# Expert tiles of a mixture of experts: the turn of the silu rows moved ahead of the next tile's gate and up products

## The chip, the cores and the metric

The kernel runs on one NeuronCore of a Trainium2 chip: TensorE (matmuls), VectorE, ScalarE, GpSimd and SyncE, which here issues most transfers. The metric is the time of one execution on the device in microseconds (us), lower is better.

## What is computed

A whole two-layer network runs in one launch: attention, feed-forward, attention and feed-forward, then a gated delta net, a mixture of experts, a linear recurrence, and the same mixture again. The change touches the mixture alone, which runs twice (`moe1`, `moe2`), on 2048 rows of 256 numbers, in float32:

```python
logits = x @ router_w
expert_idx = jnp.argmax(logits, axis=-1)
score = jax.nn.sigmoid(jnp.max(logits, axis=-1))
xs = x * score[:, None]
for e in range(n_experts):                       # 8 experts, D = F = 256
    m = (expert_idx == e)[:, None]
    xe = jnp.where(m, xs, 0.0)
    h = jax.nn.silu(xe @ gate_w[e]) * (xe @ up_w[e])
    out = out + jnp.where(m, h @ down_w[e], 0.0)
shared = jax.nn.silu(x @ shared_gate_w) * (x @ shared_up_w) @ shared_down_w
```

## The kernel before

`route_and_sort` finds each row's expert, scales the rows by the score, and scatters them with indirect transfers into a DRAM tensor `moe_xs`, sorted by expert and padded, so that each tile of 128 rows belongs to one expert. There are SL = 23 such tiles (16 full ones and 7 for the padding). Then each tile goes through its expert, and the results, in the DRAM tensor `moe_ys`, are gathered back. The shared expert of batches 0 and 1 runs ahead of the tiles (`hidden`, `down`, lines 798 to 816), that of batches 2 and 3 behind them (line 890), while GpSimd gathers (line 943).

One tile q takes these steps:

- a load of 128 KB from `moe_xs` into `moe_rows` (L783), issued by SyncE; three buffers;
- on TensorE the turn of the rows, `turn_rows` (L839, 2 matmuls against the identity), copied to `moe_rows_turned` by VectorE (L1009);
- on TensorE gate and up together, `gate_up` (L849: 4 matmuls of 512 columns in the trace); ScalarE takes the silu of the gate half (L917), VectorE multiplies it by the up half into `moe_hidden` (L1015);
- on TensorE the turn of that product, `turn_hidden` (L861, 2 matmuls), copied to `moe_hidden_turned` by ScalarE (L922);
- on TensorE the down product, `result` (L871: 4 matmuls of 256 columns), copied to `moe_result` by ScalarE (L926), and a store of 128 KB to `moe_ys` (L778), issued by SyncE.

The order on every engine is written out by hand and skewed over tiles. Each engine runs its own instructions in that order, and semaphores join the engines. TensorE's iteration q (lines 878 to 886) is: load the tile's expert number into a register, turn the rows of tile q, gate and up of tile q-1, turn the hidden rows of tile q-2, result of tile q-2. The wait ahead of `turn_hidden` is for the product of its tile (`hr`, L855), the wait ahead of `result` is for the copy of its turned rows (`htc`, L865). SyncE's iteration q (lines 780 to 785) waits until the rows of tile q-3 are turned, issues the load of tile q, then waits for the copied result of tile q-3 and issues its store. So the load of tile q+1 stands behind the store of tile q-3 in SyncE's queue. VectorE alternates the copy of tile q's turned rows with the product of tile q-1 (lines 1004 to 1015).

Of the kernel before, what the change touches and what calls it, by code (L numbers as in the profile page):

```python
# [16 lines left out]
KT = DM // P  # L17
# [708 lines left out]
def route_and_sort(nc, name, X, XN, XT, W, M, C):  # L726
# [4 lines left out]
    E, F = 8, DM  # L731
    SL = NT + E - 1
    xs_d, ys_d = M.xs_d, M.ys_d
    with Stage(nc, name) as s:
# [16 lines left out]
        HRT = [s.sb(f"hidden_turned{i}", [P, KT, P]) for i in range(2)]  # L751
# [3 lines left out]
        xtp, gup, htp, yp = B[0:2], B[2:4], B[4:6], B[6:8]  # L755
# [11 lines left out]
        @blk.sync  # L767
        def _(sp):
            sp.dma_start(rw[:, :, :], tiles(W["router"])).then_inc(ld, 16)
            sp.dma_start(tri[:, :], C.dram["before"]).then_inc(ld, 16)  # L770
            sp.dma_start(thr[:, :], C.dram["thresholds"]).then_inc(ld, 16)  # L771
            sp.dma_start(slots[:, :], C.dram["slots"]).then_inc(ld, 16)  # L772
            if M.load is not None:
                M.load(sp)

            def store(q):
                sp.wait_ge(yc, q + 1)
                sp.dma_start(ys_d[q * P:(q + 1) * P, :], YR[q % 3][:, :]).then_inc(yst[q % 3], 16)  # L778
            sp.wait_ge(scat, 16 * NT)
            for q in range(SL):  # L780
                if q >= 3:
                    sp.wait_ge(xt, q - 2)
                sp.dma_start(XR[q % 3][:, :], xs_d[q * P:(q + 1) * P, :]).then_inc(rld[q % 3], 16)  # L783
                if q >= 3:
                    store(q - 3)
            for q in range(SL - 3, SL):
                store(q)

        @blk.tensor
        def _(pe):  # L790
# [41 lines left out]
            def turn_rows(q):  # L832
                pe.wait_ge(rld[q % 3], 16 * (q // 3 + 1))
                if q < 2:
                    pe.wait_ge(silus, 2 * FIRST - 1 + q)
                else:
                    pe.wait_ge(xtc, q - 1)
                for k in range(KT):
                    mm = nc.tensor.transpose(xtp[q % 2][:, k * P:(k + 1) * P], XR[q % 3][:, k * P:(k + 1) * P], C.ident[:, :])  # L839
                mm.then_inc(xt, 1)  # L840

            def gate_up(q, e):
                if q < 2:
                    pe.wait_ge(hids, 2 * FIRST - 1 + q)
                else:
                    pe.wait_ge(hr, q - 1)
                pe.wait_ge(xtc, q + 1)
                for k in range(KT):
                    mm = nc.tensor.matmul(gup[q % 2][:, :], XRT[q % 2][:, k, :],  # L849
                                          M.wgu[:, k, ds(e, 1), :].rearrange("p a n -> p (a n)"),  # L850
                                          start=(k == 0), stop=(k == KT - 1))
                mm.then_inc(gu, 1)

            def turn_hidden(q):
                pe.wait_ge(hr, q + 1)  # L855
                if q < 2:
                    pe.wait_ge(added, TB * (FIRST - 1) + q + 1)
                else:
                    pe.wait_ge(htc, q - 1)
                for k in range(KT):  # L860
                    mm = nc.tensor.transpose(htp[q % 2][:, k * P:(k + 1) * P], HR[q % 2][:, k * P:(k + 1) * P], C.ident[:, :])  # L861
                mm.then_inc(ht, 1)

            def result(q, e):
                pe.wait_ge(htc, q + 1)  # L865
                if q < 2:
                    pe.wait_ge(added, TB * (FIRST - 1) + q + 3)
                else:
                    pe.wait_ge(yc, q - 1)
                for f in range(KT):  # L870
                    mm = nc.tensor.matmul(yp[q % 2][:, 0:DM], HRT[q % 2][:, f, :],  # L871
                                          M.wd[:, f, ds(e, 1), :].rearrange("p a n -> p (a n)"),
                                          start=(f == 0), stop=(f == KT - 1))
                mm.then_inc(yd, 1)
# [3 lines left out]
            for q in range(SL + 2):  # L878
                if q < SL:
                    chosen[q] = pe.value_load(EXP[0:1, q:q + 1], min_val=0, max_val=E - 1)  # L880
                    turn_rows(q)
                if 1 <= q <= SL:
                    gate_up(q - 1, chosen[q - 1])
                if q >= 2:
                    turn_hidden(q - 2)
                    result(q - 2, chosen[q - 2])
            pe.wait_ge(hr, SL)
            pe.wait_ge(xtc, SL)
# [7 lines left out]
        @blk.scalar  # L896
        def _(act):
            act.wait_ge(bested, 1)
            nc.scalar.activation(score[:, :], best[:, :], ACT.Sigmoid).then_inc(scored, 1)
            act.wait_ge(scored, 1)  # L900
            for t in range(NT):
                nc.scalar.activation(XN[:, t, :], XN[:, t, :], ACT.Copy, scale=score[:, t:t + 1]).then_inc(xsd, 1)

            def silu(b):
                for f in range(2):
                    act.wait_ge(gates, 2 * b + f + 1)
                    if b > 0:
                        act.wait_ge(hids, 2 * (b - 1) + f + 1)
                    nc.scalar.activation(act_sb[f][:, :], gp[f][:, :], ACT.Silu).then_inc(silus, 1)
            for b in range(FIRST):  # L910
                silu(b)
            for q in range(SL + 2):
                if 1 <= q <= SL:
                    act.wait_ge(gu, q)
                    if q >= 3:
                        act.wait_ge(hr, q - 2)
                    nc.scalar.activation(SG[(q - 1) % 2][:, :], gup[(q - 1) % 2][:, 0:F], ACT.Silu).then_inc(sg, 1)  # L917
                if q >= 2:
                    act.wait_ge(ht, q - 1)
                    if q >= 4:  # L920
                        act.wait_ge(yd, q - 3)
                    nc.scalar.copy(HRT[q % 2][:, :, :], htp[q % 2][:, 0:F].rearrange("p (k n) -> p k n", k=KT)).then_inc(htc, 1)  # L922
                    act.wait_ge(yd, q - 1)
                    if q >= 5:
                        act.wait_ge(yst[(q - 2) % 3], 16 * ((q - 2) // 3))
                    nc.scalar.copy(YR[(q - 2) % 3][:, :], yp[q % 2][:, 0:DM]).then_inc(yc, 1)  # L926
            for b in range(FIRST, BATCH):
                silu(b)
# [1576 lines left out]
```

## Time and profile before

| | us |
|---|---|
| median of 3 runs | 4703.91 |
| lowest, highest | 4699.47, 4708.26 |
| the profiled execution, whole | 4706.56 |
| its span | 4704.8 |
| tiles of `moe1` in it, first turn to the last result's start | 4210.02 to 4303.80 |
| tiles of `moe2` in it | 4568.26 to 4660.33 |

A row of the profile names a line, an engine, an operation and the tensors (out <- in). PE is TensorE's matmuls, PEld its weight loads, DVE VectorE, ACT ScalarE, SPq the transfers that SyncE issues. A matmul of 256 columns lasts 379 ns from start to end, and its successor starts before it ends, so distances between starts tell more of TensorE than durations do. The granted clock of TensorE is a share of 2.4 GHz: 1.00 is that level, 0.50 is 1.2 GHz.

### The profile page before, as it was taken

How to read it: one execution, taken by the hardware profiler on the slowest of the kernel's cores; microseconds unless marked ns; L12 is line 12 of the kernel's file. 1: busy time of each engine (PE TensorE's matmuls, PEld its weight loads, DVE VectorE, ACT ScalarE, POOL GpSimd, SP SyncE). 2: the span in 40 equal slices, each digit the busy share in tenths (PEclk: the TensorE clock that was granted, in tenths of full speed). 3: DMA queues.
4: the chain of work that ended last, by engine and by line, in shares of the span. 5: the costliest groups of instructions: out<-in, count | busy, mean ns of one | idle time of the engine just before them, and what ended most of it. 6: DMA issues, size and time to landing. Idle time of an engine off the chain costs nothing. (4 is left out here: it accounts for less than half of the span.)

```text
span 4704.8 us, 79644 instructions
## 1 busy us (share of the span) xinstructions
PE 4118.0 (88%) x27938; PEld 2752.2 (58%) x27938; DVE 2696.7 (57%) x7063; ACT 2268.6 (48%) x6183; POOL 630.6 (13%) x557
## 2 busy tenths in 40 slices
PE   5988988888797799959999999999999999977667
PEld 3555545555555566646666666666766666644344
DVE  3663357777623788856666665566556666423342
ACT  1551146666411566635556555656565565522111
POOL 0000010000000344421111111111111111111011
PEclk8788989889897899979999999999999999979879
DMA  2000100000000655553222332333233232121012
GB/s 70 1 1 24 51 1 2 2 2 2 4 27 5 206 200 205 213 134 84 79 70 74 84 84 71 81 84 83 70 84 84 66 80 79 37 92 57 11 34 76
DMA packets 402161, 318.92 MB, mean 68 GB/s; under 512 B 289200, under 2 KB 339056, under 8 KB 399728
## 3 DMA queue, kind: packets, MB, share of 16 engines
q1 hardware_dynamic: 398704, 305.53, 22.6%
q0 software_dynamic: 3072, 8.39, 0.6%
q8 instruction: 225, 3.69, 0.3%
q14 instruction: 160, 1.31, 0.1%
HBM read 195.94 MB, written 117.88 MB: 67 GB/s over the span
## 5 line engine op out<-in xcount | busy, mean ns | idle before, releaser
L2153 ACT ACTIVATE d_heads_VP<-d_heads_chain,d_GALL 128x128 f32<-128x128 f32 x512 | 187.9, 367 | 665.1 <-PE d_heads_chain L2055 663.5
L2299 DVE SCALAR_TENSOR_TENSOR d_heads_S<-d_heads_S,d_GALL,d_heads_chain 128x128 f32<-128x128 f32 x768 | 232.4, 344 | 436.0 <-PE d_heads_chain L2060 435.9
L599 ACT ACTIVATE b_heads_PR<-b_heads_sc,b_heads_NM 128x384 f32<-128x384 f32 (+3 forms) x512 | 273.0, 535 | 203.4 <-DVE b_heads_NM L667 203.4
L1763 DVE SCALAR_TENSOR_TENSOR d_front_CY<-d_front_proj,d_CW,d_front_CY 128x511 f32<-128x511 f32 (+2 forms) x384 | 274.1, 745 | 72.6 <-ACT d_front_CY L1681 68.0
L1969 PE MATMUL d_heads_value<-all_XT,d_heads_WVZ 128*128 128x512 f32 x512 | 271.1, 612 | 27.9 <-DMA d_heads_WVZ<-w_d_qkvz 27.9
L2232 POOL TENSOR_TENSOR d_heads_RM<-d_heads_MS,d_heads_mhalf 128x4 f32<-128x4 f32 x128 | 130.4, 1019 | 1199.9 <-DVE d_heads_MS L2312 1199.9
L2277 DVE SCALAR_TENSOR_TENSOR d_heads_CY<-d_heads_value,d_CW,d_heads_CY 128x511 f32<-128x511 f32 (+2 forms) x384 | 284.6, 741 | 1.8
L1990 PE MATMUL d_heads_value<-d_heads_WVZ,all_XT 128*128 128x256 f32 x1024 | 273.6, 390 | 12.0 <-DVE d_heads_CY L2277 12.0
L2087 PE MATMUL d_heads_projected<-d_heads_WO,d_heads_OT 128*128 128x256 f32 x1024 | 277.0, 394 | 0.7 <-ACT d_heads_OT L2172 0.7
L2060 PE MATMUL d_heads_chain<-d_heads_VP,d_heads_KD 64*128 64x128 f32 x1792 | 220.4, 322 | 54.2 <-ACT d_heads_VP L2153 54.1
L2291 DVE SCALAR_TENSOR_TENSOR d_heads_UU<-d_heads_chain,d_GALL,d_heads_VB 128x128 f32<-128x128 f32 x448 | 156.5, 349 | 192.9 <-PE d_heads_chain L2042 192.9
L547 PEld LDWEIGHTS b_heads_tp<-all_ident,b_heads_PR 128*128 128x128 f32 x1280 | 158.0, 156 | 170.7 <-ACT b_heads_PR L599 129.1
L2042 PE MATMUL d_heads_chain<-d_heads_S,d_heads_KQ 128*64 128x128 f32 x1792 | 249.3, 302 | 8.5 <-DVE d_heads_S L2299 2.4
L547 PE MATMUL b_heads_tp<-all_ident,b_heads_PR 128*128 128x128 f32 x1280 | 223.6, 311 | 37.2 <-DVE b_heads_PT L679 24.3
L1639 PE MATMUL d_front_proj<-all_XT,d_front_WKQ 128*128 128x512 f32 x512 | 242.4, 618 | 15.3 <-DMA d_front_WKQ<-w_d_qkvz 15.3
L2065 PE MATMUL d_heads_output<-d_heads_VP,d_heads_ITB 128*128 128x128 f32 x1024 | 244.4, 321 | 0.0
L538 PE MATMUL b_heads_sc<-b_QKT,b_heads_QM 32*128 32x128 f32 (+3 forms) x1024 | 229.3, 527 | 17.0 <-DVE b_heads_QM L635 8.9
L2060 PEld LDWEIGHTS d_heads_chain<-d_heads_VP,d_heads_KD 64*128 64x128 f32 x1792 | 134.8, 184 | 176.9 <-ACT d_heads_VP L2153 163.7
L2227 POOL TENSOR_TENSOR d_heads_QS<-d_heads_KQ,d_heads_GE 128x512 f32<-128x512 f32 x128 | 162.9, 1274 | 517.2 <-PE d_heads_output L2065 510.8
L2045 PE MATMUL d_heads_output<-d_heads_S,d_heads_QS 128*64 128x128 f32 x1792 | 226.8, 282 | 0.0
L2263 DVE TENSOR_TENSOR d_heads_TMP<-d_heads_INV 128x30 f32<-128x30 f32 (+14 forms) x480 | 209.5, 437 | 28.5 <-DMA d_heads_INV<-d_l 25.1
L2042 PEld LDWEIGHTS d_heads_chain<-d_heads_S,d_heads_KQ 128*64 128x64 f32 x1792 | 126.7, 136 | 158.5 <-DVE d_heads_S L2299 56.2
(323 smaller groups left out, 8932.3 us busy)
## 6 DMA issues: line engine op xcount, KB each, us to landing
d_kq<-d_front_KQ SPq DMA_DIRECT2D x64, 768.0 KB, 4.3
d_heads_KQ<-d_kq SPq DMA_DIRECT2D x64, 768.0 KB, 4.9
d_heads_GE<-d_gerows SPq DMA_DIRECT2D x128, 256.0 KB, 5.3
d_front_GR<-d_grows SPq DMA_DIRECT2D x32, 512.0 KB, 6.4
d_it<-d_front_LI SPq DMA_DIRECT2D x64, 256.0 KB, 2.1
d_l<-d_front_LI SPq DMA_DIRECT2D x64, 256.0 KB, 4.0
d_heads_ITB<-d_it SPq DMA_DIRECT2D x128, 128.0 KB, 2.8
d_heads_INV<-d_l SPq DMA_DIRECT2D x256, 32.0 KB
```

What stands on the lines that cost most here:

```text
L547: mm = nc.tensor.transpose(TP[j][:, k * P:(k + 1) * P], PR[p % 3][j][:, k * P:(k + 1) * P], C.ident[:, :])
L599: nc.scalar.activation(PR[p % 3][j][:, 0:width(p)], SC[p % 2][j][:, 0:width(p)], ACT.Exp, bias=NM[:, u % 2, t, slot:slot + 1], scale=-1.0 ...
L1639: mm = nc.tensor.matmul(FB[2 * (i % 2) + c][:, :], WKQ[:, k, g, col:col + HD], XT[:, k, b * SEQ:(b + 1) * SEQ], start=(k == 0), stop=(k == ...
L1763: stt(y, FB[2 * (i % 2) + c][:, 0:SEQ - j], CW[:, n, 3 - j:4 - j], y, ALU.mult, ALU.add).then_inc(convstep if j < 3 else convs, 1)
L1969: mm = nc.tensor.matmul(BV[h][:, :], w[:, k, h * HD:(h + 1) * HD], XT[:, k, b * SEQ:(b + 1) * SEQ], start=(k == 0), stop=(k == KT - 1))
L1990: mm = nc.tensor.matmul(BV[t // 2][:, (t % 2) * DM:(t % 2 + 1) * DM], XT[:, k, b * SEQ + t * P:b * SEQ + (t + 1) * P], w[:, k, 2 * HD:4 * HD],
L2042: mm = nc.tensor.matmul(R[0][hrows(h), 0:HD], kq[:, c, 0, :], S[:, h, :], start=True, stop=True)
L2060: mm = nc.tensor.matmul(R[h][:, HD:2 * HD], KD[i % 2][hrows(h), c, :], VP[c % 2][hrows(h), :], start=True, stop=True)
L2065: mm = nc.tensor.matmul(inter, ITB[i % 2][:, c, :], VP[c % 2][:, :], start=(c == 0), stop=True, skip_group_check=True)
L2087: mm = nc.tensor.matmul(BO[:, t * DM:(t + 1) * DM], OT[:, h, t * P:(t + 1) * P], WO[g % 2][:, h, :], start=(h == 0), stop=(h == 1))
L2277: stt(y, BV[h][:, 0:SEQ - j], CW[:, 2 * HK + 2 * g + h, 3 - j:4 - j], y, ALU.mult, ALU.add).then_inc(convstep if j < 3 else convs, 1)
L2299: stt(S[:, h, :], S[:, h, :], gate(i, GEL0 + h, c), R[h][:, HD:2 * HD], ALU.mult, ALU.add).then_inc(su, 1)
```

## The change

On TensorE, `turn_hidden(q - 2)` moves from behind `gate_up(q - 1)` to ahead of it. On ScalarE, the copy of the turned hidden rows of tile q-2 moves from behind the silu of tile q-1 to ahead of it; the copy of the result stays last. Waits move with their instructions; none is added or dropped. VectorE, SyncE and GpSimd keep their order. In the changed file lines behind the edit stand one or two further down: L918 is the copy that was L922, L923 the silu that was L917, L928 the copy that was L926.

```diff
@@ -879,10 +879,11 @@
                     turn_rows(q)
+                if q >= 2:
+                    turn_hidden(q - 2)
                 if 1 <= q <= SL:
                     gate_up(q - 1, chosen[q - 1])
                 if q >= 2:
-                    turn_hidden(q - 2)
                     result(q - 2, chosen[q - 2])
@@ -910,16 +911,17 @@
             for q in range(SL + 2):
+                if q >= 2:
+                    act.wait_ge(ht, q - 1)
+                    if q >= 4:
+                        act.wait_ge(yd, q - 3)
+                    nc.scalar.copy(HRT[q % 2][:, :, :], htp[q % 2][:, 0:F].rearrange("p (k n) -> p k n", k=KT)).then_inc(htc, 1)
                 if 1 <= q <= SL:
                     act.wait_ge(gu, q)
                     if q >= 3:
                         act.wait_ge(hr, q - 2)
                     nc.scalar.activation(SG[(q - 1) % 2][:, :], gup[(q - 1) % 2][:, 0:F], ACT.Silu).then_inc(sg, 1)
                 if q >= 2:
-                    act.wait_ge(ht, q - 1)
-                    if q >= 4:
-                        act.wait_ge(yd, q - 3)
-                    nc.scalar.copy(HRT[q % 2][:, :, :], htp[q % 2][:, 0:F].rearrange("p (k n) -> p k n", k=KT)).then_inc(htc, 1)
                     act.wait_ge(yd, q - 1)
```

On TensorE, in one iteration of the tile loop, the difference of the two orders (L880 loads the expert's number, the ISA rows set the weights' address from it):

```order
 L880 ISA x2
 L839 MATMUL moe_bank<-all_ident,moe_rows 128x128 x2
-L849 ISA
-L849 MATMUL moe_bank<-moe_gate_up,moe_rows_turned 128x512
-L849 ISA
-L849 MATMUL moe_bank<-moe_gate_up,moe_rows_turned 128x512
 L861 MATMUL moe_bank<-all_ident,moe_hidden 128x128 x2
+L849 ISA
+L849 MATMUL moe_bank<-moe_gate_up,moe_rows_turned 128x512
+L849 ISA
+L849 MATMUL moe_bank<-moe_gate_up,moe_rows_turned 128x512
 L871 ISA
 L871 MATMUL moe_bank<-moe_down,moe_hidden_turned 128x256
```

The gate and up products of the next tile now stand between the turn of the hidden rows (L861) and the result that needs their copy (L871); the two turns stand side by side.

On ScalarE, the first tiles of a call before:

```order
L917 ACTIVATE moe_gate_silu<-moe_bank 128x256 x2
L922 COPY moe_hidden_turned<-moe_bank 128x256
L926 COPY moe_result<-moe_bank 128x256
L917 ACTIVATE moe_gate_silu<-moe_bank 128x256
L922 COPY moe_hidden_turned<-moe_bank 128x256
L926 COPY moe_result<-moe_bank 128x256
```

And the same place after:

```order
L923 ACTIVATE moe_gate_silu<-moe_bank 128x256
L918 COPY moe_hidden_turned<-moe_bank 128x256
L923 ACTIVATE moe_gate_silu<-moe_bank 128x256
L928 COPY moe_result<-moe_bank 128x256
L918 COPY moe_hidden_turned<-moe_bank 128x256
L923 ACTIVATE moe_gate_silu<-moe_bank 128x256
L928 COPY moe_result<-moe_bank 128x256
```

The copy for the result comes ahead of the next tile's silu, in the order in which TensorE now feeds the two.

## Rows read from the trace of the kernel before

**Rows 1.** The page: busy time (share, instructions), and the last chain's start by line.

```profile
PE 4118.0 (88%) x27938; PEld 2752.2 (58%) x27938; DVE 2696.7 (57%) x7063; ACT 2268.6 (48%) x6183; POOL 630.6 (13%) x557
...
PE moe_bank L849 1%; PE moe_bank L871 1%; PE moe_bank L804 0%; PE moe_bank L814 0%; ACT moe_hidden_turned L922 0%; PE moe_bank L839 0%; DMA moe_rows<-moe_xs 0%; DVE all_X L1025 0%; ACT moe_gate_silu L917 0%; DVEq L37 0%; ACT moe_result L926 0%; SPq L770 0%; DVE all_X L999 0%; SPq L772 0%; SPq L771 0%
```

**Rows 2.** Line L871: what TensorE sat idle for before it (us, times).

```profile
  ACT moe_hidden_turned L922: 27.9, 46
```

**Rows 3.** Timeline of one tile in `moe2`: start us, duration, engine, line [idle before].

```profile
4615.68 0.38 PE L839 MATMUL moe_bank<-all_ident,moe_rows 128*128 128x128 f32 x2
...
4615.88 0.37 ACT L926 COPY moe_result<-moe_bank 128x256 f32<-128x256 f32 x1 [1.30 <-PE moe_bank L871]
4615.90 1.92 PE L849 MATMUL moe_bank<-moe_gate_up,moe_rows_turned 128*128 x4
...
4616.28 0.32 SPq L778 DMA_DIRECT2D moe_ys<-moe_result  x1
...
4616.65 0.43 SPq L783 DMA_DIRECT2D moe_rows<-moe_xs  x1
...
4617.66 0.38 PE L861 MATMUL moe_bank<-all_ident,moe_hidden 128*128 128x128 f32 x2
...
4617.86 0.38 ACT L917 ACTIVATE moe_gate_silu<-moe_bank 128x256 f32<-128x256 f32 x1 [1.61 <-PE moe_bank L849]
4618.14 0.37 ACT L922 COPY moe_hidden_turned<-moe_bank 128x256 f32<-128x256 f32 x1
4618.28 0.42 DVE L1015 TENSOR_TENSOR moe_hidden<-moe_gate_silu,moe_bank 128x256 f32<-128x256 f32 x1 [1.75 <-ACT moe_gate_silu L917]
...
4618.65 1.13 PE L871 MATMUL moe_bank<-moe_down,moe_hidden_turned 128*128 x4 [0.60 <-ACT moe_hidden_turned L922]
...
4619.61 0.38 PE L839 MATMUL moe_bank<-all_ident,moe_rows 128*128 128x128 f32 x2
```

**Rows 4.** Timelines of the shared expert: a stream without waits, and VectorE releasing TensorE.

```profile
4319.39 5.34 PE L814 MATMUL moe_bank<-moe_shared_down,moe_hid 128*128 128x256 f32 x24
...
4560.29 0.42 DVE L999 TENSOR_TENSOR all_X<-all_X,moe_bank 128x256 f32<-128x256 f32 x1 [2.45 <-PE moe_bank L814]
...
4560.77 0.73 PEld L814 LDWEIGHTS moe_bank<-moe_shared_down,moe_hid 128*128 128x128 f32 x4 [0.34 <-DVE all_X L999]
```

**Rows 5.** Landing of the loads of L783: all 46, and those issued at 4604.86 and 4632.36.

```profile
DMA to landing us min/median/max: 1.9/2.2/3.5
...
DMA to landing us min/median/max: 2.7/2.7/2.7
...
DMA to landing us min/median/max: 3.5/3.5/3.5
```

**Rows 6.** Timeline of the head of the loop in `moe2`.

```profile
4568.26 1.41 PE L839 MATMUL moe_bank<-all_ident,moe_rows 128*128 128x128 f32 x4 [3.52 <-DMA moe_rows<-moe_xs]
...
4572.51 0.38 PE L839 MATMUL moe_bank<-all_ident,moe_rows 128*128 128x128 f32 x2
...
4573.13 0.42 DVE L1015 TENSOR_TENSOR moe_hidden<-moe_gate_silu,moe_bank 128x256 f32<-128x256 f32 x1 [3.00 <-ACT moe_gate_silu L917]
...
4576.40 0.38 PE L839 MATMUL moe_bank<-all_ident,moe_rows 128*128 128x128 f32 x2
```

**Rows 7.** TensorE's timeline: turns of tiles 3 and 22 in `moe1`, 22 in `moe2`, its last result.

```profile
4219.78 0.38 PE L839 MATMUL moe_bank<-all_ident,moe_rows 128*128 128x128 f32 x2
...
4295.21 0.38 PE L839 MATMUL moe_bank<-all_ident,moe_rows 128*128 128x128 f32 x2
...
4651.68 0.38 PE L839 MATMUL moe_bank<-all_ident,moe_rows 128*128 128x128 f32 x2
...
4660.33 1.12 PE L871 MATMUL moe_bank<-moe_down,moe_hidden_turned 128*128 x4 [0.61 <-ACT moe_hidden_turned L922]
```

**Rows 8.** Stretches: from:to, length, busy us of PE, PEld, DVE, ACT, POOL; clock, DMA share, GB/s.

```profile
4219.80:4299.10 79.30, 67.21 (x241) 37.16 (x241) 16.91 (x40) 20.39 (x60) 0.00 (x0) 1.00 0.21 65
4568.00:4576.30 8.30, 7.38 (x20) 3.63 (x20) 2.82 (x8) 1.03 (x3) 0.00 (x0) 0.77 0.12 41
4576.30:4655.60 79.30, 66.77 (x242) 37.59 (x241) 16.93 (x40) 20.39 (x60) 0.00 (x0) 1.00 0.21 65
```

## The prediction, made before the changed kernel ran

> **What bounds the kernel now.** I began with the page: TensorE is busy 88% of the span, and the chain that ended last runs through the expert tiles by way of TensorE and ScalarE's copy L922 [rows 1]. That share is a mean over many stages, so I went to the stage that the change touches, and there to what ended TensorE's waits. Ahead of `result` (L871) TensorE sat idle 27.9 us in all, 46 times, until ScalarE's copy of the turned hidden rows was there [rows 2]: once per tile, 2 calls of 23 tiles.
>
> One tile's timeline shows why [rows 3]. The turn L861 starts at 4617.66, the copy L922 at 4618.14, and the result at 4618.65: 0.99 us from turn to result, of which the turn itself needs 0.22 (the other turn, L839, holds its successor back from 4615.68 to 4615.90). TensorE has nothing to do in between. The other steps by their starts: turn of rows 0.22, gate and up 1.76 (4615.90 to 4617.66), result 0.96 (4618.65 to 4619.61). Sum 0.22 + 1.76 + 0.99 + 0.96 = 3.93 us, the distance of the two turns shown. From the turn of tile 3 to that of tile 22 are 19 such distances: 75.43 us in `moe1`, 75.28 in `moe2` [rows 6, 7], 3.97 and 3.96 each. Behind the tiles both TensorE (the shared expert) and GpSimd (the gather) wait for the last tile's result, so what the loop saves leaves the path that sets the end.
>
> **What the change removes.** With gate and up between turn and result, the copy has 0.22 + 1.76 = 1.98 us of TensorE's work to hide under and needs 0.99: the wait ahead of the result goes, with 0.99 us of slack. The result, no longer started from idle, should also lose its slow start: 24 such matmuls without a wait take 5.34 us [rows 4], (5.34 - 0.38) / 23 = 0.216 apart, so 4 take 0.86 instead of 0.96. TensorE alone then needs 0.22 + 0.22 + 1.76 + 0.86 = 3.06 us a tile. If the slow start stays it is 3.16.
>
> **What is late next.** Three things move with it, and each has to be paid from rows.
>
> First, the turn of the hidden rows now needs its product sooner. Before, a whole gate-and-up product lay between; now only the result and the turn of rows do. From the start of gate and up: silu at 1.96 (4615.90 to 4617.86), product 0.42 later, 0.42 long [rows 3], and VectorE's end to TensorE's start 0.06 (4560.71 to 4560.77) [rows 4]: 2.86 us. TensorE reaches the turn at 1.76 + 0.86 + 0.22 = 2.84. So it waits some 0.02 us, and this loop closes at 2.86 + 0.22 = 3.08 us a tile. It is a tie; each 0.1 us by which the path is longer than read costs 0.1 a tile. What is queued behind this wait on TensorE is gate and up of the next tile.
>
> Second, the loads. SyncE issues the load of tile q+1 behind the store of tile q-3: 0.97 us after that tile's result gave way to the next turn (4615.68 to 4616.65) [rows 3]; it lands 2.2 us later at the median [rows 5], and TensorE needs it one iteration on. With 0.05 for the release that is 3.22 us, against 3.93 of cover before and 3.06 to 3.08 after: 0.15 short. A turn that comes late does not delay the result that stands before it, so the next load is issued as early as ever and finds a longer cover: late and punctual turns alternate, and the mean is (3.08 + 3.22) / 2 = 3.15. This transfer was not waited for in a usual tile, so its price is bounded: 3.08 if every load lands in 2.1 us or less, (3.08 + 1.02 + 2.7) / 2 = 3.40 if every load takes the 2.7 that the second slowest takes [rows 5]. I take 2.2, the median of 46, since two transfers of 128 KB a tile keep the engines busy only 0.21 of the time [rows 8]. Every second tile then restarts from idle, for up to 0.10: 3.15 + 0.05 = 3.20 us a tile.
>
> The Trainium skill ("DMA: Bandwidth & Descriptors", Anatomy of one DMA) puts a near constant 2.0 us on a transfer, and its fit (for transfers that GpSimd issues) would give 2.3 for 128 KB; with it the mean would be 3.20 before the restart, 2 us more over both calls. The trace's median is 2.2.
>
> Third, ScalarE's order. The silu now stands behind the wait for the turn, but the turn comes 1.98 us ahead of the silu's own input, so nothing is late. The copy of the result runs from 0.20 to 0.57 after the turn of rows starts [rows 3], the next copy of hidden rows is due at 0.22 + 0.48 = 0.70: no conflict. The expert number's load into TensorE's register now runs ahead under gate and up as before under the result: nothing. VectorE and GpSimd keep order and load: nothing.
>
> **Head and tail.** In iteration 2 the turn of tile 0's hidden rows must wait for a product that ends at 4573.13 + 0.42 = 4573.55 [rows 6]: TensorE idles from 4572.73 to 4573.61. The next turn of rows then comes at 4573.61 + 0.22 + 1.76 + 0.86 = 4576.45, against 4576.40: 0.05 us lost and no gain for that tile. At the end, from the turn of tile 22 to the last result were 8.65 us (4651.68 to 4660.33) [rows 7]. Now: two turns 0.44, gate and up to the next hidden turn 2.86, turn 0.22, again 2.86, and the last turn to result 0.99, uncovered as before: 7.37. That saves 1.28.
>
> **The sum.** 19 distances in each call: 75.43 + 75.28 - 38 x 3.20 = 150.7 - 121.6 = 29.1. Tails 2 x 1.28 = 2.6, heads -0.1. A load of 3.5 us, one in this execution [rows 5], costs up to 0.9 more than before, as its cover shrank by that: -0.9. Together 30.7 us. The profiled execution took 4706.56, which gives 4675.9; it lies 2.65 above the median of the three runs, so against that median I forecast 4673.2.
>
> **Rivals.** (A) The loads set the pace: with less cover and stores of the same rate, landings go to 2.5 to 2.7 us. For it: single loads of 2.7 and 3.5 exist, and both 128 KB transfers now come every 3.2 us. Against: DMA share 0.21. At 3.40 a tile: 150.7 - 129.2 + 1.6 = 23.1, so 4680.8. (B) A wait in place of the one removed: the product reaches the turn later than 2.86, say 0.25 us late each time, 3.33 a tile: 150.7 - 126.5 + 1.6 = 25.8, so 4678.1. The tie speaks for it; that each step of the path is read from rows speaks against more. (C) It does nothing that can be measured: that needs 3.9 - 0.25 = 3.7 us a tile, a path from gate and up to turn of 3.5, 0.6 us longer than its rows. Time 4697 to 4704. (D) Slower, through the clock. TensorE's first turns, after 3.52 us of idle, ran long (1.41 us for 4, against 0.38 for 2), and the granted clock of the head was 0.77, that of the steady stretches 1.00 with 0.60 us of idle in each tile [rows 6, 8]. The change puts 0.88 us of idle into the head, just where the clock has come up from its lower level, 1.2 GHz. If that level returned and stayed, a tile would need about 2 x 3.06 = 6.1 us, 2.15 more than now and 2.9 more than forecast: from 30.7 / 2.9, some 11 of the 46 tiles on, the kernel is slower; with 16, 4703.9 - 30.7 + 46.4 = 4720. Against it: 0.60 us of idle per tile leaves 1.00 granted, and the change ends most idle time.
>
> The Trainium skill ("TensorE: Matmul & The Clock Gate", Part 1) says that the throttled clock is the default and activity releases it, which by itself would favour a loop with fewer gaps. The trace agrees on the busy stretches, which were granted 1.00.
>
> **How the numbers follow.** Forecast (3.08 to 3.28 a tile) 0.72, A 0.12, B 0.09, C 0.05, D 0.02. Range: its low end is TensorE alone at 3.06, 150.7 - 116.3 + 2.5 = 36.9, so 4667, less some 2 for the runs' own spread of 4.4 either way; its high end takes in A and B, 4681, with 4 for the spread and 2 for both at once. 4665 to 4687. A measurement of this kernel can tell about 0.2%, 9.4 us, from no change; faster by more than that is the forecast with A and B, 0.93, no change 0.05, slower 0.02.
>
> **What would show it.** In the profile after, turns of rows 3.1 to 3.3 us apart, L871 with no idle time but at each call's last tile (under 2 us in all for 46), L839 waiting for `moe_rows` loads about every second tile by 0.1 to 0.3, L861 waiting for VectorE's product by under 0.1. Rival A shows as landings over 2.4 in the median and waits at L839 of 0.4 and more; B as waits at L861 of 0.2 and more; C as turns still 3.8 apart; D as a granted clock under 1.00 in the tiles. I am wrong if the loop stays above 3.4.

## The result and the profile after

| kernel | median, us | lowest to highest | runs | profiled run | its span | granted clock |
|---|---|---|---|---|---|---|
| before | 4701.69 | 4696.35 to 4708.26 | 4 | 4706.56 | 4704.8 | 0.919 |
| after | 4661.17 | 4657.25 to 4669.32 | 4 | 4669.32 | 4667.5 | 0.919 |

The ratio is 0.9915, 95% interval 0.9896 to 0.9935: faster, by 40.5 us or 0.85%. I had forecast 4673.2 in a range of 4665 to 4687. The sign was right; the time lies 3.8 us below the range.

The profile answers first on the loop. On the page, TensorE is busy 12 us less than before, its weight loads as long as before, and the span is 37 us shorter [rows 1]; ScalarE's copy of the turned hidden rows, which stood high in the chain, is gone from the lines that the page shows of it.

```profile
PE 4106.2 (88%) x27938; PEld 2751.5 (59%) x27938; DVE 2696.8 (58%) x7063; ACT 2273.0 (49%) x6183; POOL 629.5 (13%) x557
...
PE moe_bank L849 1%; PE moe_bank L871 0%; POOL moe_xs L939 0%; PE moe_bank L794 0%; POOL all_XN L945 0%; PE moe_bank L804 0%; DMA moe_rows<-moe_xs 0%; PE moe_bank L839 0%; PE moe_bank L861 0%; DVE all_X L1027 0%; DMA all_XN<-moe_ys,moe_pos 0%; DMA moe_xs<-all_XN,moe_pos 0%; DMA moe_slots<-c_slots 0%; DMA moe_ys<-moe_result 0%; DVE moe_hidden L1017 0%
```

What TensorE sat idle for (us, times), ahead of the result L871, of the turn of hidden rows L861 and of the turn of rows L839, one line of each line's own view:

```profile
  ACT moe_hidden_turned L918: 1.1, 2
```

```profile
  DVE moe_hidden L1017: 5.2, 8
```

```profile
  DMA moe_rows<-moe_xs: 42.6, 42
```

The 27.9 us ahead of the result [rows 2] are 1.1, and those belong to the last tile of each call. L861 waits only in the first and the last tiles of the calls. L839 waited for loads 21.7 us, 8 times, before; now it is 42.6 us, 42 times. That view counts a weight load (PEld) and its matmul apart: 35 of the 46 turns of rows show such a wait, 5 did before. The loads have become what is late.

One tile and the start of the next in `moe2`, start and duration in us, in the form of [rows 3]:

```profile
4599.81 0.44 PE L839 MATMUL moe_bank<-all_ident,moe_rows 128*128 128x128 f32 x2
...
4600.09 0.38 PE L861 MATMUL moe_bank<-all_ident,moe_hidden 128*128 128x128 f32 x2
...
4600.31 1.88 PE L849 MATMUL moe_bank<-moe_gate_up,moe_rows_turned 128*128 x4
...
4600.51 0.37 ACT L918 COPY moe_hidden_turned<-moe_bank 128x256 f32<-128x256 f32 x1 [0.17 <-PE moe_bank L861]
...
4600.73 0.43 SPq L783 DMA_DIRECT2D moe_rows<-moe_xs  x1
...
4602.03 1.03 PE L871 MATMUL moe_bank<-moe_down,moe_hidden_turned 128*128 x4
...
4602.64 0.42 DVE L1017 TENSOR_TENSOR moe_hidden<-moe_gate_silu,moe_bank 128x256 f32<-128x256 f32 x1 [1.93 <-ACT moe_gate_silu L923]
...
4602.90 0.20 PEld L839 LDWEIGHTS moe_bank<-all_ident,moe_rows 128*128 128x128 f32 x2 [0.25 <-DMA moe_rows<-moe_xs]
4602.91 0.44 PE L839 MATMUL moe_bank<-all_ident,moe_rows 128*128 128x128 f32 x2
...
4603.18 0.38 PE L861 MATMUL moe_bank<-all_ident,moe_hidden 128*128 128x128 f32 x2
```

The copy L918 starts at 4600.51 and is needed at 4602.03, so it lies under gate and up. Turn to turn is 4602.91 - 4599.81 = 3.10 us, where [rows 3] had 3.93. The product ends at 4602.64 + 0.42 = 4603.06, 0.12 before the next L861.

The stages by the starts of the turns. "Ahead" is the part of the program before the first turn of `moe1`, which no kernel here changes; a call runs from its first turn to the start of its last result; a distance is the mean of the 19 from tile 3 to tile 22.

| profile | ahead | distance `moe1` / `moe2` | tail, each call | both calls | last result to end | span |
|---|---|---|---|---|---|---|
| before | 4210.0 | 3.970 / 3.962 | 8.59 / 8.65 | 185.85 | 44.47 | 4704.8 |
| after | 4208.4 | 3.201 / 3.268 | 7.44 / 7.44 | 154.66 | 40.38 | 4667.5 |
| e1, before again | 4214.0 | 3.972 / 3.968 | 8.59 / 8.66 | 184.85 | 40.33 | 4701.2 |
| e2, after again | 4205.7 | 3.352 / 3.182 | 7.43 / 7.44 | 155.88 | 40.34 | 4666.3 |
| e7, after | 4212.9 | 3.359 / 3.237 | 7.44 / 7.44 | 157.11 | 40.52 | 4674.8 |
| e11, after | 4209.3 | 3.444 / 3.143 | 7.40 / 7.40 | 156.76 | 40.36 | 4669.2 |
| e3, turn alone | 4202.5 | 4.129 / 4.126 | 8.97 / 9.05 | 194.11 | 40.35 | 4700.9 |
| e4, copy alone | 4210.9 | 3.915 / 3.931 | 8.49 / 8.47 | 182.57 | 40.31 | 4697.0 |
| e5, loads first | 4209.1 | 3.114 / 3.113 | 7.44 / 7.44 | 149.90 | 40.41 | 4661.8 |
| e6, before with loads first | 4216.4 | 3.972 / 3.969 | 8.59 / 8.65 | 184.88 | 40.38 | 4703.7 |
| e10, loads first again | 4207.1 | 3.113 / 3.113 | 7.44 / 7.44 | 150.08 | 40.39 | 4659.8 |
| e8, turns swapped | 4204.7 | 3.884 / 3.884 | 7.24 / 7.23 | 182.37 | 40.40 | 4690.6 |
| e9, swapped, number ahead | 4209.2 | 3.470 / 3.383 | 7.13 / 7.13 | 162.36 | 40.42 | 4674.5 |
| e12, number three times | 4210.0 | 3.453 / 3.468 | 7.39 / 7.37 | 166.80 | 40.90 | 4678.7 |

The four profiles of the changed kernel (after, e2, e7, e11) have 154.7 to 157.1 us in the two calls, mean 156.1, against 185.85 and 184.85: 28.8 to 29.8 us gone, where the sum said 30.7. The rest of the 40.5 us is not in the tiles.

### The profile page after: what moved, and what is told of

It reads as the page before. It is cut to its first block and busy times, and to the rows that moved or that the text cites. A ratio compares the mean times of both kernels' runs of the same rounds, so it can differ in the third digit from the quotient of the medians.

```text
span 4667.5 us, 79644 instructions
## 1 busy us (share of the span) xinstructions
PE 4106.2 (88%) x27938; PEld 2751.5 (59%) x27938; DVE 2696.8 (58%) x7063; ACT 2273.0 (49%) x6183; POOL 629.5 (13%) x557
```

## The experiments

**e1 and e2: the two kernels again**, without an edit, side by side.

> The kernel before, unchanged, profiled a second time. In the first profile VectorE's adds of the shared expert (L999, 32 of them) sat idle 36 us in all, 2.3 to 4.6 us at a time, while GpSimd issued indirect transfers; in the profile of the changed kernel the same adds sat idle 12.4 us and never over 0.5 at a time, in all four places, also where the code ahead of them is the same. Theory P (the built program decides it, by its layout or by what the change does to the timing): the gaps are back here, L999 idle 30 to 40 us, L814 with waits, and the stretch from the last result to the last add again 34.2 us in the second call. Theory X (each execution draws it): the adds may well run 0.86 apart here, idle about 12 us, and the span is then some 7 us shorter than 4704.8. The tile loops: 3.96 us a tile as before under both.

> The changed kernel, unchanged, profiled a second time and timed in five rounds. Loop theory: 3.15 to 3.3 us a tile again (60 to 62.5 us for the 19 distances of each call), which is worth 31 us. Theory P: L1001 idle about 12 us again and none over 0.5, so the ratio stays near 0.9915 (about 40 us): 31 in the loops and 7 behind them. Theory X: here the adds may show gaps of 2 us and more, and with more runs the ratio moves towards 31 us, 0.9934.

Measured: e1 4698.13 (10 runs), ratio 1.0005 [0.9995, 1.0015] to before; e2 4669.71 (5 runs) against 4694.5, ratio 0.9947 [0.9933, 0.9960]. That interval just touches the first one's. The gain is 25 us here and was 40 there, with the same two programs. VectorE's adds sat idle 12.4 us in e1 as in e2, against 36 in the first profile of the same program, so theory X holds: the long gaps belong to that one execution, not to the program. The stage table shows where such a difference can sit: the unchanged part ahead of the tiles ended anywhere from 4202.5 to 4216.4 us over all the profiles, while the calls of one kernel agree within 2.5 us.

**e3 and e4: one half of the change each.** e3 moves the turn on TensorE and leaves ScalarE's order; e4 moves the copy on ScalarE and leaves TensorE's.

```diff
 e3 (TensorE)
+                if q >= 2:
+                    turn_hidden(q - 2)
                 if 1 <= q <= SL:
                     gate_up(q - 1, chosen[q - 1])
                 if q >= 2:
-                    turn_hidden(q - 2)
                     result(q - 2, chosen[q - 2])
 e4 (ScalarE)
+                if q >= 2:
+                    act.wait_ge(ht, q - 1)
...
+                    nc.scalar.copy(HRT[q % 2][:, :, :], htp[q % 2][:, 0:F].rearrange("p (k n) -> p k n", k=KT)).then_inc(htc, 1)
                 if 1 <= q <= SL:
                     act.wait_ge(gu, q)
...
```

> TensorE's half of the change alone: the turn of the hidden rows ahead of gate and up, ScalarE's copies in the old order, silu first. The copy of the turned rows then waits behind a silu that waits for gate and up. Theory of the prediction (the gain needs both halves): result waits for silu at 1.92 us after gate and up start, copy 0.28 behind, result 0.51 behind that, 2.71 against a cover of 1.72, so L871 idles about 1.0 us a tile (45 us in all) and a tile takes 0.22 + 0.22 + 2.7 + 0.96 = 4.1 us: 5 to 8 us slower than before, near 4708. Rival (the shorter stream with both turns side by side is itself the gain): L871's idle time falls and the kernel is faster than before by 10 us and more. Adds of L999: under P whatever this program gives, no forecast; under X either.

> ScalarE's half of the change alone: the copy of the turned hidden rows ahead of the next silu, TensorE in the old order. Theory of the prediction: the result still follows the turn directly, with 0.99 us between their starts less the little that the silu held the copy back (turn to copy 0.42 where nothing is ahead of it in the changed kernel, against 0.48): L871 idles 0.54 a tile, 25 us in all, a tile takes 3.90, and the time is 0 to 3 us below the kernel before, within 0.1%. The silu comes later by at most 0.5 us, which a whole gate and up product hides. Rival (the order on ScalarE was the wait): L871's idle time falls to a few us and the time by 20 us and more.

Measured: e3 4711.63 (5 runs), ratio 1.0039 [1.0026, 1.0052]; e4 4698.58 (10 runs), ratio 1.0001 [0.9992, 1.0011]. e3's timeline in `moe2`:

```profile
4600.19 0.38 ACT L918 ACTIVATE moe_gate_silu<-moe_bank 128x256 f32<-128x256 f32 x1 [1.78 <-PE moe_bank L849]
4600.47 0.37 ACT L923 COPY moe_hidden_turned<-moe_bank 128x256 f32<-128x256 f32 x1
...
4600.98 1.12 PE L871 MATMUL moe_bank<-moe_down,moe_hidden_turned 128*128 x4 [0.82 <-ACT moe_hidden_turned L923]
```

The turn had started at 4598.05, 2.4 us ahead of its copy, but the copy stood behind the silu, which waits for gate and up. The turn is early and its copy is late: TensorE waits 0.82 us in each tile. In sum ahead of L871, of e3 and then of e4:

```profile
  ACT moe_hidden_turned L923: 37.5, 46
```

```profile
  ACT moe_hidden_turned L917: 25.3, 46
```

Against 27.9 before [rows 2], e3 waits 9.6 us more and e4 2.6 less. By the two calls, e3's half alone loses 8 to 9 us, e4's gains 2 to 3, and both together gain some 29: ahead of the silu the copy finds the turned rows, and only then does gate and up cover it. e3's time rose by 17 us (interval 12 to 24) where its loops account for 8 to 9; the rest is not in the tiles of its profile. Four of its five runs had a granted clock of 0.918 or 0.919; what that goes with is shown below.

**e5, e6 and e10: loads a tile earlier.** SyncE issued the store of tile q-3 ahead of the load of tile q+1. This edit takes the store one iteration later, so that the load no longer stands behind a store that waits for the newest result. e5 and e10 make it in the changed kernel, e6 in the kernel before.

```diff
-                if q >= 3:
-                    store(q - 3)
-            for q in range(SL - 3, SL):
+                if q >= 4:
+                    store(q - 4)
+            for q in range(SL - 4, SL):
                 store(q)
```

> The changed kernel, with SyncE's store one iteration later: the load of tile q+1 then stands behind the store of tile q-4, a whole tile earlier. Theory (the loads are what holds the changed loop above TensorE's own pace, by the waits of 0.2 to 1.4 us ahead of L839): those waits go but for the first tiles, a tile takes 3.06 to 3.12, the 19 distances 58.5 to 59.5 us instead of 60.5 to 63.7, each call 2 to 4 us less, 4 to 6 us less in all than the changed kernel: about 36 us under the kernel before. A load of 3.7 us is then hidden too. Rival (the late turns were covered by the wait for VectorE's product, which now shows instead): L861 waits 0.1 and more in each tile and the 19 distances stay over 60.

> The same edit of SyncE's order in the kernel before, where a load has 3.9 us of cover. Theory: no load but a rare one over 2.9 us is waited for there, so nothing changes beyond a few tenths: 3.93 to 3.97 us a tile, same time as before within 0.1%. Rival (the loads, or the expert numbers' register load, cost the old loop something all along): 19 distances well under 74.7, a gain of 2 us and more.

> The version with the loads a tile earlier, again, beside the changed kernel on one chip. Its tile loops took 149.9 us for both calls against 154.7, 155.9 and 157.1 of the changed kernel's three profiles, but the two medians were equal (4665.9 and 4665.8). Theory (the loops' 6 us are real and the medians' own spread of some 6 us hid them): 149 to 151 us again, and a median 2 to 9 us under that of the changed kernel. Rival (something outside of the tiles gives them back): equal medians again with loops of 150.

Measured: e5 4665.87 (6 runs), ratio 0.9935 [0.9922, 0.9947]; e10 4668.23 (5 runs), 0.9932 [0.9918, 0.9946]; e6 4701.67 (10 runs), 1.0009 [0.9999, 1.0018]. e5's turns of rows in `moe2`, then what TensorE waited for ahead of L839:

```profile
4595.27 0.38 PE L839 MATMUL moe_bank<-all_ident,moe_rows 128*128 128x128 f32 x2
...
4598.39 0.38 PE L839 MATMUL moe_bank<-all_ident,moe_rows 128*128 128x128 f32 x2
...
4601.50 0.27 PE L839 MATMUL moe_bank<-all_ident,moe_rows 128*128 128x128 f32 x1
```

```profile
  DMA moe_rows<-moe_xs: 24.0, 6
```

Of the 42 rows of waits, the 6 at the heads are left, and the distances are an even 3.11 to 3.12. What sets 3.11 is not separated: the product of the tile ends 0.06 us before the turn of hidden rows starts (4601.67 to 4601.73), the release time of [rows 4], so VectorE's path and TensorE's own work meet there, as the first step said. Both calls take 149.90 us (150.08 in e10), 6 us less than the changed kernel's 156.1. In e6 the same edit moves nothing: 184.88 against 184.85. The loads bind only once the copy is covered. By time the 6 us can't be told: e10 is 6.1 us below e11, with intervals that overlap, and e5 0.1 above e7. It is the best version by its trace; by its time no difference is shown.

**e7 and e11: the changed kernel, beside e5 and beside e10.**

> The changed kernel a third time, beside the two others on one chip. The two timings so far disagree (0.9915 and 0.9947) while the tile loops of their profiles agree (154.7 and 155.9 us for both calls, against 185.9 and 184.9 before). Theory (the change is worth what the loops show, 30 us; the rest is what each execution draws in the 4200 us ahead of the tiles): loops of 153 to 157 us, and a ratio between 0.992 and 0.995, near 0.9936. Rival (a real effect outside of the loops, 10 us more): near 0.9915 again.

> The changed kernel a fourth time, for the comparison with the version whose loads come a tile earlier. Loops of 154 to 158 us for both calls; ratio 0.992 to 0.995.

Measured: e7 4665.77 (6 runs), ratio 0.9936 [0.9922, 0.9950]; e11 4674.31 (5 runs), 0.9941 [0.9927, 0.9955]. With the first result and e2 the ratios are 0.9915, 0.9947, 0.9936, 0.9941. Their mean by runs (4, 5, 6, 5) is 0.9936, where e7's expectation had put it; its rival, a real effect of 10 us outside of the loops, would have given 0.9915 again.

**e8 and e9: the turn of hidden rows ahead of the turn of rows.** The two turns change places. In e8 the load of the expert's number into TensorE's register goes with the turn of rows, behind the turn of hidden rows and its wait; in e9 it stays ahead of both.

```diff
 e8
+                if q >= 2:
+                    turn_hidden(q - 2)
                 if q < SL:
                     chosen[q] = pe.value_load(EXP[0:1, q:q + 1], min_val=0, max_val=E - 1)
                     turn_rows(q)
-                if q >= 2:
-                    turn_hidden(q - 2)
 e9
                 if q < SL:
                     chosen[q] = pe.value_load(EXP[0:1, q:q + 1], min_val=0, max_val=E - 1)
-                    turn_rows(q)
                 if q >= 2:
                     turn_hidden(q - 2)
+                if q < SL:
+                    turn_rows(q)
```

> The changed kernel with TensorE's two turns swapped: hidden rows of tile q-2, then the rows of tile q. Work is the same; the turn of hidden rows comes 0.22 us sooner after gate and up of its tile. Theory (the path from gate and up over silu and product to that turn is 2.8 to 2.9 us, and it is met almost to the point in the changed kernel): TensorE arrives at 1.72 + 0.86 = 2.58 and waits 0.25 to 0.3 in every tile, so the loop closes at 2.86 + 0.22 + 0.22 = 3.30 to 3.35 us and the load's wait is hidden under it: 19 distances of 63 to 64 us, 3 to 5 us slower than the changed kernel in all. Rival (the path has slack): 60.5 to 62 us as in the changed kernel, no waits at L861.

> The order of the previous experiment (hidden rows turned first, then the rows of tile q), but the load of tile q's expert number into TensorE's register stands ahead of both turns instead of between them. There the turn of rows came 0.75 us behind the turn of hidden rows, where two turns side by side are 0.22 to 0.28 apart, and a tile took 3.88 us. Theory (TensorE's own instruction stream stops at the wait for VectorE's product, and the register load behind it can only then begin, some 0.5 us in the open): the turns are again 0.22 to 0.28 apart, a tile takes 2.89 + 0.25 + 0.22 = 3.35 us, 19 distances 63 to 64.5 us, and the kernel is 18 to 22 us faster than in the previous experiment, some 3 slower than the changed kernel. Rival (the 0.5 us belong to the wait for the rows' load or to the copies): still 3.8 to 3.9 us.

Measured: e8 4696.76 (10 runs), ratio 1.0004 [0.9992, 1.0015], 3.88 us a tile; e9 4677.55 (4 runs) against 4698.68, 0.9955 [0.9939, 0.9970], 3.30 in a usual tile. e8's timeline:

```profile
4592.73 1.96 PE L849 MATMUL moe_bank<-moe_gate_up,moe_rows_turned 128*128 x4
...
4595.15 0.42 DVE L1017 TENSOR_TENSOR moe_hidden<-moe_gate_silu,moe_bank 128x256 f32<-128x256 f32 x1 [1.79 <-ACT moe_gate_silu L923]
...
4595.62 0.44 PE L861 MATMUL moe_bank<-all_ident,moe_hidden 128*128 128x128 f32 x2
...
4596.37 0.41 PE L839 MATMUL moe_bank<-all_ident,moe_rows 128*128 128x128 f32 x2 [0.31 <-issue]
...
4596.61 1.96 PE L849 MATMUL moe_bank<-moe_gate_up,moe_rows_turned 128*128 x4
```

The first step is as forecast: from gate and up to the hidden turn are 4595.62 - 4592.73 = 2.89 us, the path that I had summed as 2.86. The second is not: 0.75 us from that turn to the turn of rows, where 0.28 separates them in the changed kernel (4599.81 to 4600.09). e8's expectation missed by 0.5 us a tile. The register load of e8 starts just with the turn of hidden rows (4595.62), behind the wait, and the next weight load comes at 4596.34. Its rows, from a window around that turn:

```profile
L882 PEldq TENSOR_LOAD <-moe_expert x1: 298/298/298, 4595.6 to 4595.6; - x1
L882 PEldq FUSED_REGOPS  x1: 151/151/151, 4596.0 to 4596.0; - x1
```

e9 keeps everything but the place of the register load:

```profile
4582.23 0.44 PE L861 MATMUL moe_bank<-all_ident,moe_hidden 128*128 128x128 f32 x2
4582.51 0.38 PE L839 MATMUL moe_bank<-all_ident,moe_rows 128*128 128x128 f32 x2
4582.72 1.88 PE L849 MATMUL moe_bank<-moe_gate_up,moe_rows_turned 128*128 x4
...
4585.53 0.44 PE L861 MATMUL moe_bank<-all_ident,moe_hidden 128*128 128x128 f32 x2
```

0.28 between the turns and 3.30 a tile: the half microsecond was the register load, started only once the wait ahead of it was over. e9's two calls are still longer than the changed kernel's (162.4 us against 156.1), because the loop has the hidden path (from gate and up at 4582.72 to the next turn at 4585.53: 2.81 us) plus both turns with nothing beside them. By time e9 lies 3.2 us above e11, with intervals that overlap.

**e12: the expert's number loaded three times**, six more instructions per tile on TensorE with the same matmuls and transfers, to tell what the slow loads follow (see below).

```diff
                 if q < SL:
-                    chosen[q] = pe.value_load(EXP[0:1, q:q + 1], min_val=0, max_val=E - 1)
+                    for _ in range(3):
+                        chosen[q] = pe.value_load(EXP[0:1, q:q + 1], min_val=0, max_val=E - 1)
                     turn_rows(q)
```

> The changed kernel with each tile's expert number loaded into TensorE's register three times instead of once: 6 more instructions in TensorE's stream per tile, on the 31 that the order shows (24 weight loads and matmuls, 4 ISA rows, 3 for the number). In the profiles so far the slow loads of L783 (3.1 to 4.1 us against 2.2) came 7 or 8 tiles apart, before the change as after it, and each beside one packet of 16 KB on the instruction queue q8. Theory (that packet is the next piece of TensorE's instruction stream, so it comes after a number of instructions, and it delays the load that it meets): slow loads and q8 packets come 6 to 6.5 tiles apart. If the three register loads (about 0.5 us each) fit under gate, up and result, a tile without a slow load takes 3.1 to 3.2 us as before; if not, up to 3.6. Rival (they follow time or some other engine's stream): still 7 to 8 tiles, or 23 us, apart.

Measured, one run, so that nothing is said of its time: 4680.46, both calls 166.80 us, 3.40 in a usual tile. The instruction packets came 6.2 to 6.5 tiles apart, as the theory had it (last section). The register loads did not quite fit beside the matmuls; ahead of L839 TensorE was idle 20.8 us for "issue", as in these two tiles:

```profile
4251.83 0.41 PE L839 MATMUL moe_bank<-all_ident,moe_rows 128*128 128x128 f32 x2 [0.26 <-issue]
...
4255.23 0.41 PE L839 MATMUL moe_bank<-all_ident,moe_rows 128*128 128x128 f32 x2 [0.19 <-issue]
```

## Why the steps of the prediction held and its range did not

**What held.** The result lost its wait (1.1 us in 2 places, forecast under 2). The tail is 7.44 us where the steps gave 7.37. The heads of e1's 8.12 and 8.62 became 8.2 and 8.7, the 0.05 that was forecast. The first profile of before has 9.76 in `moe1`'s head; that was an exception. TensorE's idle time in the head, which I had feared for the clock, was 0.71 us (forecast 0.88). The stretches of that head and of the tiles behind it, in `moe1`: length, the busy times of the engines in the order of [rows 8], granted clock, DMA share, GB/s:

```profile
4208.40:4216.60 8.20, 7.38 (x20) 3.80 (x21) 1.79 (x5) 1.14 (x3) 0.00 (x0) 0.78 0.13 37
4216.60:4277.40 60.80, 59.90 (x230) 35.06 (x228) 16.06 (x39) 21.45 (x57) 0.00 (x0) 1.00 0.27 83
```

The tiles were granted 1.00, as before [rows 8]: rival D fell. Rival B (a new wait for the product) fell with the 8 waits at L861, none in a usual tile. Rival C fell with a mean of 3.27 us a tile over four profiles. Rival A, a general slowing of the transfers, fell too: the landings kept their median, 2.1 us after against 2.2 before [rows 5].

```profile
DMA to landing us min/median/max: 1.9/2.1/3.7
```

The Trainium skill ("DMA: Bandwidth & Descriptors", Anatomy of one DMA) would have had 2.3 by its fit, for transfers that GpSimd issues; these loads, issued by SyncE, take 2.1 to 2.2 for 128 KB, and the sum by the trace's own median was the better one.

Punctual and late turns alternate in some stretches, as the second step said. TensorE's turns of rows in one of `moe1`:

```profile
4236.20 0.44 PE L839 MATMUL moe_bank<-all_ident,moe_rows 128*128 128x128 f32 x2
...
4239.28 0.38 PE L839 MATMUL moe_bank<-all_ident,moe_rows 128*128 128x128 f32 x2
...
4242.49 0.44 PE L839 MATMUL moe_bank<-all_ident,moe_rows 128*128 128x128 f32 x2
...
4245.57 0.38 PE L839 MATMUL moe_bank<-all_ident,moe_rows 128*128 128x128 f32 x2
...
4249.24 0.44 PE L839 MATMUL moe_bank<-all_ident,moe_rows 128*128 128x128 f32 x2 [0.40 <-DMA moe_rows<-moe_xs]
```

Distances 3.08, 3.21, 3.08: a mean of 3.145 for a pair, where I had 3.20 with a restart from idle. More turns wait than the every second one that I forecast (35 of 46), but the punctual ones among them by some 0.2 us at the weight load alone. In other stretches they are even (3.10 us from 4599.81 to 4602.91, with a wait of 0.25 us at the weight load alone), so a usual tile takes some 3.10 to 3.15, and the restart cost next to nothing. e5, without these waits, has 3.113.

**The term of the sum that was mis-sized** is the slow load. I had booked one load of 3.5 us for 0.9 us, since the profile before held one such load. The four profiles of the changed kernel hold 2 to 5 loads of 2.9 us and more each, and those of 3.1 to 4.1 us make their tile 1.0 to 1.9 us longer, for example in `moe2` of after and in e11:

```profile
4584.24 0.44 PE L839 MATMUL moe_bank<-all_ident,moe_rows 128*128 128x128 f32 x2 [1.42 <-DMA moe_rows<-moe_xs]
```

```profile
4252.72 0.44 PE L839 MATMUL moe_bank<-all_ident,moe_rows 128*128 128x128 f32 x2 [1.74 <-DMA moe_rows<-moe_xs]
```

The mean distance over the four is 3.273; the 135 of the 152 that are under 3.45 us have a mean of 3.14. The 17 longer ones cost (3.273 - 3.14) x 38 = 5.1 us in place of 0.9, of which 14 loads of 2.9 us and more make 4.7, and (3.20 - 3.14) x 38 = 2.3 came back from the usual tiles: 1.9 us less gained than forecast. The two calls say the same, 184.85 - 156.1 = 28.8 in place of 30.7. That the sum came so near is in part luck: an error of 4.2 us was half covered by one of 2.3 the other way. The slow loads are also more than before, and not only less covered: 2 to 5 in a profile, against 1 in the first profile of before and none in e1. The last section shows what changed for them.

**The step that failed** is the low end of the range, by the width that I gave the runs. I took TensorE alone, 4667, "less some 2 for the runs' own spread of 4.4 either way", and set all of it against a median of three runs. Over four comparisons the medians of before were 4701.69, 4694.5, 4697.33 and 4698.68, by their runs (4, 22, 23, 9) 4696.8; those of the changed kernel 4661.17, 4669.71, 4665.77 and 4674.31, by their runs 4668.0. The miss of 4673.2 - 4661.2 = 12.0 then divides in three: the median of three from which I started, 4703.9, lay 7.1 above 4696.8; the changed kernel's four first runs lay 6.8 below 4668.0; and the gain was 28.8 instead of 30.7, 1.9 the other way. 7.1 + 6.8 - 1.9 = 12.0. Pooled, the changed kernel stands at 0.9936 (the ratios) to 0.9939 (the medians) of before, and 4668.0 lies within the range. The mechanism and its sum held to 2 us. The 2 us that I allowed for the spread should have been some 7 at each of the two medians: the median of three stood in for the kernel before, though it lay 7.1 us off.

**What the spread goes with.** The part ahead of the tiles, the same instructions in all kernels, differs by 14 us between profiles. The runs show that it goes with TensorE's granted clock. Of the 65 runs of the kernel before in e1 to e12 whose clock is on record, the 12 with a mean of 0.919 took 4703.5 us on average, the 9 with 0.922 took 4691.4; of the 20 of the changed kernel, the 7 with 0.919 took 4669.6 and the 6 with 0.921 took 4663.0. The profiles place it: between 1500 and 2500 us, long before the tiles, e6 and e1 were granted 0.92 and reached the tiles last (4216.4, 4214.0), e3 and e8 0.93 and reached them first (4202.5, 4204.7). One hundredth of the clock over those 1000 us would be some 10 us by my estimate. At an equal clock (0.919, 0.920, 0.921) the changed kernel's runs average 30 to 34 us less than those of the kernel before, near what the loops show, and e3's five, with a mean of 0.919 and 4710.5 us, lie 7 us above the 4703.5. That is a correlation; what makes the clock differ there no run tells.

**What stays open.** The first profile of before needed 44.47 us behind its last result, all others 40.3 to 40.9. Its adds (L999) show it; above, what VectorE waited for ahead of them in that profile and one of the adds, below the same lines of after:

```profile
  PE moe_bank L814: 18.3, 10
  remote: 17.4, 6
...
4684.15 0.42 DVE L999 TENSOR_TENSOR all_X<-all_X,moe_bank 128x256 f32<-128x256 f32 x1 [3.14 <-remote]
```

```profile
  PE moe_bank L814: 12.4, 28
...
4646.37 0.42 DVE L1001 TENSOR_TENSOR all_X<-all_X,moe_bank 128x256 f32<-128x256 f32 x1 [0.44 <-PE moe_bank L814]
```

It makes 4.1 of the 6.1 us by which the difference of the two first spans, 37.3, exceeds that of their calls, 31.2; another 1.6 lie ahead of the tiles. GpSimd issued the gather's indirect transfers there, but it did so in the other profiles too, which show 12.4. The Trainium skill ("SBUF — State Buffer", Who interferes with whom) would not expect an add with one input in PSUM to contend with GpSimd. One profile in fourteen can't say what else it was.

## What to carry to other kernels

When two engines hand a tile back and forth (turn on TensorE, copy on ScalarE), put the next tile's long product between the hand-over and its use, on both engines: e3's calls lost 8 us by doing it on one. Then ask which transfer had been hidden by the old wait, and look at its slowest landings as well as its median; here one store issued one iteration later removed all its waits but those at the heads (6 us in the trace, not told apart by time). And before a range is set for a change of 0.6%, ask how far medians of an unchanged kernel lie apart: here by 9 us for the kernel before (4694.5 to 4703.9) and 13 for the changed one, a third of the gain and more.

## What the runs showed of the hardware

**Slow loads come beside a fetch of instructions.** One 16 KB packet of the instruction queue q8 passes the DMA engines every seven or so tiles, and a load that was issued shortly before it lands late. Queue lines and the loads' landing, of e11 between 4249 and 4253 us, and between 4240 and 4249 us, where there is none (the 3.1 is the median of two loads, 4.0 and 2.1):

```profile
q8 instruction: 1, 0.02, 1.4%
...
moe_rows<-moe_xs SPq DMA_DIRECT2D x2, 128.0 KB, 3.1
```

```profile
moe_rows<-moe_xs SPq DMA_DIRECT2D x3, 128.0 KB, 2.2
```

The 14 profiles hold 84 such packets beside the tiles and 644 loads. All 32 loads of 2.9 us and more stand beside a packet, and none of the others took over 2.8 us. But not every packet makes a load late; it depends on when it comes:

| packet begins | packets | landing of the load, us |
|---|---|---|
| 0 to 1.4 us after the issue of the load | 29 | 2.75 to 4.1, all |
| 1.6 us or more after the issue, load still in flight | 19 | 2.1 to 2.7, but for one of 2.9 and one of 4.0 |
| with no load in flight | 36 | of a load issued within 1 us behind it, at most 2.8, but for two of 3.0 and 3.1 |

In the two profiles of the kernel before, only 2 of the 12 packets began with a load in flight, most some 0.9 us ahead of an issue; in the four of the changed kernel it is 20 of 24. So the change not only took cover from the loads, it also moved them under the packets. In e8 five packets met a load in flight, all of them 1.67 us or later, and no load was slow.

The packets follow how many instructions TensorE works through, not the time: 7.5 tiles or 29.9 us apart on average before (before, e1), 7.5 tiles or 29.1 us in e8, 7.3 tiles or 23.9 us in the changed kernel, and 6.3 tiles or 21.8 us in e12, with six instructions more per tile on TensorE alone. That the packet is what delays the load is argued from this timing; no run took the packet away alone. e12's, in `moe2` between 4571.5 and 4575 us:

```profile
q8 instruction: 1, 0.02, 1.6%
q14 instruction: 1, 0.01, 0.8%
...
moe_rows<-moe_xs SPq DMA_DIRECT2D x1, 128.0 KB, 3.8
```

The second instruction queue there, q14, sends 8 KB packets; the 18 loads that had one of them in flight, and none of q8, landed in 2.05 to 2.31 us.

**A register load behind a wait costs half a microsecond.** e8 against e9: 0.75 against 0.28 us between the turns, 3.88 against 3.30 us a tile. Ahead of the wait the same instructions cost nothing that can be seen; three times as many, in e12, cost 0.2 to 0.3 a tile even there.
